# Differential attention layer on one core: attention rows split straight from the transposes' PSUM bank, second map scaled by ScalarE and added by GpSimd, query products in a bank of their own

## The reference

```python
A1 = einsum('bhqd,bhkd->bhqk', Q1, K1) * scaling
A2 = einsum('bhqd,bhkd->bhqk', Q2, K2) * scaling
attn = softmax(A1) - lam * softmax(A2)
O = einsum('bhqk,bhkd->bhqd', attn, V)
rms = sqrt(mean(O * O, axis=-1, keepdims=True) + EPS)
O = O / rms * rms_scale * (1.0 - LAMBDA_INIT)
out = einsum('bne,de->bnd', O.transpose(0, 2, 1, 3).reshape(B, N, H * 2 * dh), Wo)
```

## Time and profile before

| | |
|---|---|
| median of 3 runs | 1045.73 us (1043.45 to 1045.77) |
| the profiled execution | 1053.84 us, span 1052.1 us |
| mean granted TensorE clock | 0.925 of full |
| busy: PE, DVE, ACT, POOL | 890.3, 766.6, 581.0, 793.4 us |
| from 225 to 325 us: busy PE, DVE, ACT, POOL | 98.84, 80.46, 66.07, 84.36 us; clock 1.00 |
| from 800 to 840 us: busy PE, DVE, ACT, POOL | 33.25, 27.23, 18.94, 31.60 us; clock 0.96 |

### The profile page before, as it was taken

One profiled execution on the slowest core, in us unless ns is written; L12 is line 12 of the kernel. 1 busy time (PEld: TensorE's weight loads), 2 busy tenths in 40 slices (PEclk: granted clock), 3 DMA queues, 4 the chain that ended last, 5 costly groups with the idle time before them and its releaser, 6 DMA issues.

```text
span 1052.1 us, 15341 instructions
## 1 busy us (share of the span) xinstructions
PE 890.3 (85%) x4365; PEld 720.4 (68%) x4366; DVE 766.6 (73%) x1185; ACT 581.0 (55%) x1090; POOL 793.4 (75%) x875
## 2 busy tenths in 40 slices
PE   6789999999999999999999999999999741258710
PEld 5567778887887788778877887878788531146510
DVE  6678778877887878788778878888788548536504
ACT  3546667666766576656766666766676331124300
POOL 2567888887988798888888888888799753375881
PEclk9899999999999999999999999999999955569955
DMA  2000000000000000000000000100000142011334
GB/s 70 1 11 11 1 1 19 3 1 0 20 0 0 10 10 0 0 10 10 0 0 10 10 0 0 50 0 0 1 1 1 53 130 65 19 51 26 33 35 122
DMA packets 36000, 20.67 MB, mean 20 GB/s; under 512 B 4560, under 2 KB 34416, under 8 KB 35968
## 3 DMA queue, kind: packets, MB, share of 16 engines
q1 hardware_dynamic: 30336, 15.95, 5.4%
q0 software_dynamic: 5632, 4.33, 3.0%
HBM read 13.85 MB, written 6.42 MB: 19 GB/s over the span
## 4 chain that ended last, share of the span: by engine, by line
PE 53%; issue 18%; DVE 16%; POOL 5%; ACT 3%; DMA 2%; another core or an unknown queue 2%; DVEq 0%; POOLq 0%; ACTq 0%; SPq 0%
PE t_ps L1074 7%; DVE negmax L760 6%; PE ring_a L1007 5%; PE ring_b L1007 5%; PE ring_a L1009 5%; PE ring_a L1008 5%; PE ring_b L1009 4%; PE ring_b L1008 4%; PE u_ps L1007 4%; PE u_ps L1008 4%; PE u_ps L1009 4%; POOL acc_dram L500 3%; ACT prob L572 2%; PE o_ps L1007 2%
## 5 line engine op out<-in xcount | busy, mean ns | idle before, releaser
L459 POOL TENSOR_TENSOR at_lo<-at,at_hi 128x1024 fp32r<-128x1024 f32 x127 | 308.6, 2430 | 0.8
L572 ACT ACTIVATE prob<-ring_a,negmax 128x1024 f32<-128x1024 f32 x128 | 142.8, 1116 | 252.7 <-DVE negmax L760 252.7
L431 POOL TENSOR_TENSOR s1sq<-psum 128x1 f32<-128x1 f32 x127 | 104.2, 820 | 125.2 <-ACT at L580 123.1
L828 DVE SCALAR_TENSOR_TENSOR attn<-prob,coef 128x1024 f32<-128x1024 f32 x128 | 180.1, 1407 | 5.1
L760 DVE TENSOR_REDUCE negmax<-ring_b 128x1 f32<-128x1024 f32 x128 | 155.6, 1216 | 4.7 <-PE ring_b L1009 1.7
L760 DVE TENSOR_REDUCE negmax<-ring_a 128x1 f32<-128x1024 f32 x128 | 155.7, 1216 | 1.3 <-PE ring_a L1009 0.2
L572 ACT ACTIVATE prob<-ring_b,negmax 128x1024 f32<-128x1024 f32 x128 | 142.8, 1116 | 20.3 <-DVE negmax L760 17.8
L434 POOL TENSOR_SCALAR at_hi<-at 128x1024 fp32r<-128x1024 f32 x127 | 141.4, 1114 | 0.0
L1074 PE MATMUL t_ps<-ident,attn 128*128 128x128 f32 x1024 | 134.4, 274 | 3.5 <-DVE attn L828 3.1
L1074 PEld LDWEIGHTS t_ps<-ident,attn 128*128 128x128 f32 x1024 | 118.9, 141 | 26.2 <-DVE attn L828 12.1
L580 ACT ACTIVATE at<-t_ps 128x1024 f32<-128x1024 f32 x128 | 130.2, 1017 | 2.7 <-PE t_ps L1074 2.7
(11 more groups left out here) (241 smaller groups left out, 1709.8 us busy)
## 6 DMA issues: line engine op xcount, KB each, us to landing
at<-in_L_ffn_w SPq DMA_DIRECT2D x16, 256.0 KB, 3.2
xres<-in_L_attn_X SPq DMA_DIRECT2D x2, 512.0 KB, 4.5
wq_s<-in_L_attn_Wq SPq DMA_DIRECT2D x8, 128.0 KB, 2.1
wk_s<-in_L_attn_Wk SPq DMA_DIRECT2D x8, 128.0 KB, 2.2
wv_s<-in_L_attn_Wv SPq DMA_DIRECT2D x8, 128.0 KB, 2.1
wo_s<-in_L_attn_Wo SPq DMA_DIRECT2D x8, 128.0 KB, 2.4
acc_dram<-zero SPq DMA_DIRECT2D x1, 1024.0 KB, 5.1
xg_dram<-xres SPq DMA_DIRECT2D x2, 512.0 KB, 3.4
```

The source lines that it names most:

```text
L431: pool.tensor_tensor(s1sq[:, r % TPH:r % TPH + 1], s1, s1, ALU.mult).then_inc(s1sq_ready, 1)
L459: pool.tensor_tensor(at_lo[:, g, :, c], src, at_hi[:, g, :, c].bitcast(F32), ALU.subtract).then_inc(at_split, 1)
L572: act.activation(prob[:, par, m, :], ring[m][:, :], ACT.Exp, bias=negmax[:, par, m:m + 1], accum_out=sums).then_inc(prob_ready, 1)
L828: dve.scalar_tensor_tensor(out=attn[:, par, :], in0=prob[:, par, 1, :], scalar=coef[:, par:par + 1], in1=prob[:, par, 0, :], op0=ALU.mult, ...
```

## The change

The copy of `t_ps` to SBUF (`at32`) is gone. The transposes are two halves of four blocks, in one bank of `t_ps`; ACT writes `at_hi` straight from it and DVE `at_lo`. The second map is multiplied with `coef` in place by ACT, POOL adds the two maps into `attn` (now four buffers), and POOL also makes `rs2` (a power of -1) and `coef`. The other bank of `t_ps`, `x_ps`, takes the query, `m` and weight products, a 512-column piece a slot. The pipeline is longer: the second exponential of a tile comes one slot later on ACT, the transposes at lags 3 and 4, `u` at 8, the output at 13.

```diff
-    LAG_T = 1
-    LAG_U = 6
-    LAG_O = 10
-    LAG_Y = 11
-    AT_QB, AT_WT, AT_WP, AT_M, AT_QA = (1, 2), 4, 6, 9, (11, 13)
+    LAG_E = 1
+    LAG_C = 1
+    LAG_T1 = 3
+    LAG_T2 = 4
+    LAG_U = 8
+    LAG_O = 13
+    LAG_Y = 13
+    X_QB = {0: (0, 0), 1: (1, 0), 2: (0, 1), 4: (1, 1)}
+    X_M, X_WT, X_WP, AT_WW = 5, 6, 8, 13
+    X_QA = {9: (0, 0), 10: (1, 0), 12: (0, 1), 13: (1, 1)}
+        x_ps = t_ps[:, NC:2 * NC]
 # POOL
-                    pool.tensor_scalar(at_hi[:, g, :, c], src, 1.0, 0.0, ALU.mult, ALU.add).then_inc(at_hi_done, 1)
+                    need(pool, scaled_ready, tc - 1)
+                    pool.wait_ge(prob_ready, 2 * tc + 2)
+                    pool.tensor_tensor(rs2[:, par:par + 1], psum2[:, par:par + 1], neg_one[:, :],
+                                       ALU.pow).then_inc(rs2_ready, 1)
+                    pool.tensor_tensor(coef_1[:, par:par + 1], rs2[:, par:par + 1], psum1[:, r % TPH:r % TPH + 1],
+                                       ALU.mult).then_inc(coef_1_ready, 1)
+                    pool.tensor_tensor(coef[:, par:par + 1], coef_1[:, par:par + 1], neglam_h[:, :],
+                                       ALU.mult).then_inc(coef_ready, 1)
-                    pool.tensor_tensor(at_lo[:, g, :, c], src, at_hi[:, g, :, c].bitcast(F32),
-                                       ALU.subtract).then_inc(at_split, 1)
+                    need(pool, t_ready, 2 * (ts - AB + 1))
+                    pool.wait_ge(scaled_ready, ts + 1)
+                    pool.tensor_tensor(attn[:, r % AB, :], prob[:, sp, 1, :], prob[:, sp, 0, :],
+                                       ALU.add).then_inc(attn_ready, 1)
 # ACT, the order of a slot
-                    act.activation(at32[:, r % 2, :], t_ps[:, :], ACT.Copy).then_inc(t_copied, 1)
+                at_high(0, LAG_T1 + 1)
+                exponential(1, LAG_E)
+                if not tail and i - 1 in X_QB:
+                    q_round(h, "b", *X_QB[i - 1], x_ps)
...
+                at_high(1, LAG_T2)
+                exponential(0, 0)
+                    act.wait_ge(coef_ready, tc + 1)
+                    act.activation(prob[:, par, 1, :], prob[:, par, 1, :], ACT.Copy,
+                                   scale=coef[:, par:par + 1]).then_inc(scaled_ready, 1)
 # DVE
+                        dve.tensor_tensor(at_lo[:, g, k, c], t_ps[:, 0:NC].rearrange("p (k q) -> p k q", q=P),
+                                          at_hi[:, g, k, c].bitcast(F32), ALU.subtract).then_inc(at_split, 1)
-                    dve.reciprocal(rs2[:, par:par + 1], psum2[:, par:par + 1]).then_inc(rs2_ready, 1)
-                    dve.tensor_scalar(coef[:, par:par + 1], rs2[:, par:par + 1], psum1[:, i:i + 1],
-                                      neglam_h[:, :], ALU.mult, ALU.mult).then_inc(coef_ready, 1)
-                    dve.scalar_tensor_tensor(out=attn[:, par, :], in0=prob[:, par, 1, :],
-                                             scalar=coef[:, par:par + 1], in1=prob[:, par, 0, :],
-                                             op0=ALU.mult, op1=ALU.add).then_inc(attn_ready, 1)
 # PE
+                        if half == 0:
+                            pe.wait_ge(attn_ready, tt + 1)
+                        need(pe, at_split, 2 * tt + half)
+                        for k in range(GT):
+                            kk = half * GT + k
+                            last_t = pe.transpose(t_ps[:, k * P:(k + 1) * P], attn[:, r % AB, kk * P:(kk + 1) * P],
+                                                  ident[:, :])
```

More of the change, by code:

```diff
@@ L752, in head_lambda @@
                     dve.tensor_copy(neglam_h[:, :], neglam[:, bass.ds(h, 1)]).then_inc(lam_head, 1)
-                if i == 0 and not first:
-                    head_lambda()
                 def row_max(m):
+                    par = i % 2
                     dve.wait_ge(scores_ready, 2 * t + m + 1)
@@ new lines, in output @@
+                def output():
+                    r = i - LAG_O
+                    if exists(h, r, first) and r < TPH:
+                        tt, j = t - LAG_O, r % GT
+                        g = GPH * h + r // GT
+                        if j == 0:
+                            pe.wait_ge(u_split, g + 1)
+                        if r == 0:
+                            pe.wait_ge(ww_installed, 2 * (h + 1))
+                        if not tail:
+                            need(pe, y_added, tt)
+                        elif i == TPH:
+                            pe.wait_ge(prob_ready, 2 * H * TPH)
+                        elif i >= TPH + 4:
+                            pe.wait_ge(y_added, tt - 3)
+                        q = slice(j * P, (j + 1) * P)
+                        three(o_bank(r, last)[:, 0:WWN], u_hi[:, q], u_lo[:, q],
+                              ww_hi[:, :], ww_lo[:, :]).then_inc(o_ready, 1)
@@ L1064, in slot @@
+                if not tail:
+                    scores(0, 0)
                 if first and i == 0:
```

445 lines of the change are left out of this document (204 added, 241 removed).

## The result

The changed kernel takes 1014.47 us, the median of 4 runs (1011.95 to 1015.86), beside 1045.26 us (1043.45 to 1045.77) of the kernel before on the same chip: ratio 0.9706, 95% interval 0.9683 to 0.9729. In a second comparison, on another chip, it was 1022.73 to 1049.71 us, ratio 0.9713 (0.9683 to 0.9742); the two medians alone would give 0.9743. The forecast was 1016.5.

What follows compares the result with a forecast made beforehand. TensorE, 85% busy, was taken as the busiest engine, with 4.7 us of waits a looped head and a chained first head. Loop -21, first head -15, start +1, tail +6: -29 from 1045.7, so 1016.5 us, range 1004 to 1029.

Steps and rivals of the forecast that it cites:

- the loop: Slots 16 to 127: exponentials take 669.5 us instead of 690.3, at 96.5 us a head, -21 us.
- the tail: Last exponential a to last `y`: 35.8 us instead of 30.0, with three slots of 4.3, +6 us.
- signs named ahead: If right: head 96 to 97 us, no TensorE product waits, GpSimd one-column operations near 0.2, last `y` some 36 us after.
- the 95.3: TensorE's work in a looped head without waits: 16 slots 88.6, query products 5.5, weight products 1.2 us.
- The split of the transposes: TensorE: eight transposes in two fours cost up to 0.08 us a slot, 1.3 a head; half taken, 0.7.
- narrow waits: TensorE in the loop: waits of 0.1 to 0.2 us in four or five slots, 0.5 us a head.
- The first head: First exponential to that of slot 16: 87 us instead of 102.5, a chain all in order, -15 us.
- D: Tail: stops of 1.4 us lower the clock, some 24 matmuls cost about twice, +5, 1021 us; forecast with D 0.66.
- The rest: Behind the attention (experts, top-k): not touched by the change, no term in the sum.
- B: GpSimd and ScalarE together set the slot; head stays at 99 to 100 us, total 1031 to 1038; chance 0.17.
- C: ScalarE becomes the bound: slot 6.4 us, head 102.4, total 1062, slower; chance 0.14.
- E: The split does nothing measurable: the head gains just what the tail loses; within 0.3%, 3 us; chance 0.03.

Runs made afterwards that it cites:

- distance: Kernel before with four attention buffers and transposes two slots behind the scores instead of one, later lags one slot longer: 1051.61 us, ratio 1.0068.
- row one slot late: Kernel before with four attention buffers, transposes two slots behind, and reciprocal, coefficient and fused row one slot later on VectorE: 1037.21 us, ratio 0.9949.
- a slot of distance taken back: Changed kernel with every distance behind the addition one slot shorter (transposes 2 and 3, `u` 7, output 12): 1028.60 us, ratio 0.9778.
- the norm's order: Changed kernel with a second bank for tail transposes, and the first layer norm's five steps at tail slots 20, 22, 22, 23, 25: 1007.59 us, ratio 0.9662.
- row on VectorE: Changed kernel with the fused row back on VectorE, no scale pass on ScalarE and no addition on GpSimd: 1016.27 us, ratio 0.9726.
- pieces in score bank: Changed kernel with the four query pieces of map 0 a head back in the score bank, copied first in the next slot: 1054.33 us, ratio 1.0097.
- more on ScalarE: Changed kernel with two extra 512-column copies at the end of each of ScalarE's 128 slots: 1034.19 us, ratio 0.9910.
- more on GpSimd: Changed kernel with one extra 512-column addition behind the wide one in each GpSimd slot: 1029.79 us, ratio 0.9882.
- two tail banks: Changed kernel with half 1 of the transposes in the second bank in the last head, from row 8 on: 1009.20 us, ratio 0.9673.
- shorter, banks, order: Changed kernel with distances one slot shorter, a second bank for tail transposes and the layer norm's steps at other tail slots: 1019.96 us, ratio 0.9714.

## Why the prediction was right, and where it was not

**The sum: close in part by luck.** -29 us was forecast and -30.8 measured, but two parts missed by more than the whole, in opposite directions: the loop gained 29.2 to 29.4 where 21 was said, and the tail lost 10.5 to 12.7 where 6 was said. Two of the signs named ahead also came out otherwise: a head at 95.66, under the 96 to 97, and the last row 40.5 and 42.7 us behind the last exponential a, not some 36. The direction, the order of the parts and the absence of TensorE's waits in the loop are the prediction's own.

**The loop: right mechanism, term too small.** 96.5 us a head was forecast, 95.66 measured. TensorE's list of waits over the 111 slots holds, for the changed kernel, one of 0.2 us. Two costs that were put on top of the 95.3 are not there. The split of the transposes was given 0.7 us a head. In the timeline (303.15 for the four, 303.50, 303.82 for the next) a group takes 0.35 and its follower is 0.32 from its next: twice 0.35 + 0.09 is 0.88, and eight in one took 0.79 + 0.08. It is free. The narrow waits, 0.5 a head, are 0.2 us over the 111 slots by the list. The rest of the difference, -29.4 against -21, is the last head: it makes no query pieces for a next one, four of 0.69, or 2.8 us, and the forecast took all 111 slots at one price.

**What the loop gained by** was told as one thing, the waits for a shared bank. Before, the list of waits over the 111 slots has 5.4 us for the score banks (`prob` 2.9 and 1.1, `wot_s` 1.4) and 2.5 for `u_lo`, far less than the 29.4 gained, so the list alone doesn't show the cause. The ladder of kernels divides the 4.2 us: distance 0.3 lost, row one slot late 1.5, then 2.6 for the halves, own bank and new order together, 0.4 for taking the row off VectorE. Own bank and order within the 2.6 are not separated: the old transposes fill both banks of `t_ps`, so the own bank needs the halves. The halves without it were run only for four pieces in the new order (101.07), which is above the kernel before, so that price can't be carried over to the old order. That these four pieces need a bank of their own in the new order is shown; how much of the 2.6 the bank gave is not.

**The first head: right size, wrong chain.** Forecast -15, measured -17.2. The prediction put it as "a chain: scores, maximum, exponential, attention row, transposes, all in order". The runs say that the transposes were outside: more distance left 101.6, the row one slot late took 4.1, the new order and own bank another 10.5. And the prediction took the 102.5 us for one even chain, where the slots without a product took 5.3 to 5.9 and those with one up to 9.3; the four named above hold 14.4 of the gain. So most of it is the bank's and the new order's together, and the prediction spoke of the bank for the loop only. Some of the 17.2 may be no gain: with lags of 8 and 13 instead of 6 and 10 the first head has two slots of `u` less (2 x 1.38) and three outputs less (3 x 0.52), which the tail has more. That is 4.3 us of TensorE's work at most, an estimate from TensorE's prices; with a slot of distance taken back (1.9 by the same prices) the first head was 86.1, between the two profiles of the changed kernel (85.3 and 86.6), so how much of it shows in time is open.

**The tail: right mechanism, term too small.** +6 forecast, +10.5 and +12.7 measured, and each tail slot cost 4.20 where 4.3 was worked out. What was left out is around them:

```profile
772.52 0.45 PE L1013 MATMUL ring_b<-ww_hi,u_hi 128*128 128x384 f32 x1 [1.78 <-ACT prob L579]
...
802.22 0.44 PE L1013 MATMUL ring_a<-ww_hi,u_hi 128*128 128x384 f32 x1 [3.40 <-DVE u_lo L835]
```

The tail's outputs go to the score banks, and the first waits 1.78 us for the last exponential b, which the change put one slot later. The second stop for `u_lo` was taken at 2 and is 3.40, since ScalarE's square and VectorE's row sum of the layer norm stand ahead of `u_hi` and `u_lo`; the norm's order took that away.

The rival with a falling clock (D) came true in part, and the first profile hides it. There the granted clock stays at 1.00 until the last outputs. In the second profile, behind the same waits of 1.78 and 1.13 us, it falls to the 1.2 GHz level. The two windows rows (first profile, then second) and two neighbours of the second:

```profile
774.00:782.00 8.00, 5.80 (x30) 4.29 (x30) 3.46 (x7) 4.32 (x11) 4.01 (x6) 1.00 0.01 2
```

```profile
776.00:784.00 8.00, 6.42 (x22) 4.97 (x21) 2.33 (x4) 3.78 (x9) 4.39 (x9) 0.57 0.01 2
```

```profile
777.89 0.63 PE L1014 MATMUL u_ps<-at_lo,xk_hi 128*128 128x512 f32 x1
778.31 0.63 PE L1015 MATMUL u_ps<-at_hi,xk_lo 128*128 128x512 f32 x1
```

The matmuls start 0.43 us apart instead of 0.23, and the tail is 42.7 instead of 40.5: 2.2 us, where D had put 5 for 24 matmuls. The same fall stands at this place in the profiles of the four other kernels with this tail (row on VectorE, pieces in score bank, more on ScalarE, more on GpSimd; tails 42.0 to 43.3), and not in the two with two tail banks and this distance. Why the first profile was spared is open.

**The rest** was forecast at 0, and between two profiled executions with a long rest it is 0.5 (208.6 against 208.1). The profiled execution of before had 208.1 there, and 8.21 us of them are one wait between two experts that the profile gives no releaser for:

```profile
943.89 0.79 PE L1007 MATMUL ring_a<-xk_hi,at_hi 128*128 128x512 f32 x1 [8.21 <-issue]
```

That it stood 8 us above its median was seen, and subtracting it was right.

**The rivals.** B (GpSimd and ScalarE in a closed loop) didn't occur in the looped heads: with 1.30 us a slot added on GpSimd they cost 0.05 more a slot. In the first head, where slots 1 to 11 of the changed kernel take 4.8 to 5.7 us, the same addition cost 7.9. C (ScalarE as the bound) came only with 1.3 us more a slot; where below that it begins wasn't run. E didn't occur. The prediction's rule on elementwise work is the Trainium skill's (GPSIMD Engine Reference, Performance versus the Vector engine), which has GpSimd about twice as slow. The trace agrees in price, 2.40 us on GpSimd against 1.28, and not in consequence: the kernel with the row on VectorE was not the faster one, since neither engine is what TensorE waits for.

## What to carry to other kernels

Look for a circle inside one engine's own order before looking at the lags between engines: an engine that waits, in its slot, for what it has just released paces the slot although its busy share is 73%. Then look at the slots one by one: the mean of 6.4 us in the first head hid four slots of 8.0 to 9.3, in which a product shared a bank with the scores, and most of the gain was there. A longer pipeline is not free when the head and tail are not in the loop: it moves work from the first head into the tail, where waits are bare. Here a slot of distance made the tail 4.2 to 6.5 us longer and the first head 0.8 to 1.4 shorter, and in each case the order of an engine in the tail or in the loop had its share. Taking it back worked only when the pieces that share an engine were placed anew. With TensorE 99.8 to 100% busy, moving one row between the other engines moved nothing that the ratios show; the order and the banks did. And a sum that fits should be checked part by part: here two parts missed by 4.5 to 8.4 us each and largely cancelled.

## What the runs showed of the hardware

- VectorE's fused row with two SBUF inputs takes 1.28 us when GpSimd is quiet or starts behind it, but longer where it starts into a running wide GpSimd operation. One of its two groups in the kernel with the row one slot late, then its group with the row on VectorE in the changed kernel:

```profile
L829 DVE SCALAR_TENSOR_TENSOR late<-prob,coef 128x1024 f32<-128x1024 f32 x64 | 110.6, 1727 | 2.8
```

```profile
L839 DVE SCALAR_TENSOR_TENSOR attn<-prob,coef 128x1024 f32<-128x1024 f32 x128 | 163.5, 1277 | 0.0
```

  GpSimd's subtraction beside the first stays at 2.42 in the mean; it takes 2.99 where it starts 0.55 us behind the row's start. So the one that comes second pays. The Trainium skill (GPSIMD Engine Reference, Specifications) names this contention for instructions with two SBUF inputs, and the trace agrees; who pays is from these rows.
- The same the other way round, in the changed kernel's tail: GpSimd's one-column power takes 1.62 us instead of 0.55, beside VectorE's last step of the norm.

```profile
804.84 1.62 POOL L465 TENSOR_TENSOR fac<-var_o,neg_half 128x1 f32<-128x1 f32 x1
```

- ScalarE's scale pass (pointer operand, SBUF to SBUF, 1024 columns) takes 1.156 us, taken at 1.15; the half copies 0.600 and half subtractions 0.688 from PSUM, the power of -1 on one column 0.552, GpSimd's addition 2.400.
- Behind the attention an execution costs 198.8 to 201.5 us or 208.1 to 208.6, whatever the kernel. In the second level (three of the 14 executions) TensorE stands 3 to 8 us between two experts, and the profile names no releaser. What it is stays open; it is why one profiled execution should not be compared with another without looking where their difference lies. Those waits alone don't make the level: the kernel "shorter, banks, order" has two of them, 2.90 and 4.93 us, and is at 199.5.
